# Gate stage of a mixer-and-experts kernel: load order of rows, state weights and last weight tiles; block 1's rows copied straight to the mixer's tile

## What is computed

```
xn  = (x - mean(x)) / sqrt(var(x) + eps)                       # row by row
mixer(xn):  proj = xn @ W_in.T                                 # 512 -> 2 x 1024
            u = silu(conv4(proj[:1024]) + conv_b); g = proj[1024:]
            h[t] = 0.95 h[t-1] + 0.05 (u @ W_B.T)[t]           # 64 states
            y = (h @ W_C.T + D * u) * silu(g)
            layernorm(y @ W_out.T + xn, ln_gamma, ln_beta)
experts(xn): scores = (tanh(xn @ gate_w.T) + 1) / 2            # 8 experts
            each expert takes its 1024 best rows: layernorm, fc1, gelu, fc2,
            times the score, added back to xn's rows
out = x + mixer(xn) + experts(xn)
```

## Time and profile before

| | us |
|---|---|
| median of 3 runs | 2635.19 (2635.17 to 2637.68) |
| the profiled execution's own time | 2637.41 |
| its span, first to last instruction | 2635.5 |
| PE (matmul) busy | 2606.3 |
| DVE busy | 2079.5 |
| ACT busy | 1481.2 |
| POOL busy | 675.0 |

### The profile page before, as it was taken

How to read it: one execution, slowest core, us unless ns; L and a number is a source line. 1 busy time by engine, 2 the same in 40 slices (tenths; PEclk the granted TensorE clock), 3 DMA queues, 4 the chain that set the end, 5 groups by cost and what they waited for, 6 DMA issues and landing times.

```text
span 2635.5 us, 38833 instructions
## 1 busy us (share of the span) xinstructions
PE 2606.3 (99%) x11592; PEld 2112.6 (80%) x11592; DVE 2079.5 (79%) x3570; ACT 1481.2 (56%) x2536; POOL 675.0 (26%) x1006
## 2 busy tenths in 40 slices
PE   8999999999999999999999999999999999999998
PEld 4588888888888888888888888888888888888886
DVE  8778888888888888887877778878788787887754
ACT  5744545555455656655544555565555655556553
POOL 5422222222222222213533213223132231312101
PEclk9999999999999999999999999999999999999999
DMA  9733222233333222335447436364363643636313
GB/s 367 265 128 111 76 92 87 89 104 112 112 112 112 79 85 85 96 104 166 136 125 195 109 117 161 92 155 127 117 160 93 153 131 115 159 92 156 98 56 72
DMA packets 262638, 329.62 MB, mean 125 GB/s; under 512 B 142032, under 2 KB 142160, under 8 KB 258640
## 3 DMA queue, kind: packets, MB, share of 16 engines
q1 hardware_dynamic: 228816, 230.91, 28.2%
q0 software_dynamic: 33664, 96.75, 14.9%
HBM read 259.14 MB, written 68.45 MB: 124 GB/s over the span
## 4 chain that ended last, share of the span: by engine, by line
PE 85%; DVE 10%; issue 2%; ACT 1%; DMA 1%; SPq 0%; POOL 0%; DVEq 0%; POOLq 0%; ACTq 0%
PE ring L1584 9%; PE ring L1585 9%; PE ring L1586 9%; PE po L2564 5%; PE po L2565 5%; PE po L2566 5%; PE po L1622 4%; PE pb L2565 4%; PE pb L2566 4%; PE pb L2564 4%; PE po L1623 4%; PE po L1624 4%; PE pc L2565 2%; PE pc L2566 2%; PE pc L2564 2%
## 5 line engine op out<-in xcount | busy, mean ns | idle before, releaser
L1584 PE MATMUL ring<-xt_h,w_h 128*128 128x512 f32 x1024 | 400.1, 391 | 0.1
L2564 PE MATMUL po<-w2h,hid_h 128*128 128x512 f32 x1024 | 399.3, 390 | 0.8
L1585 PE MATMUL ring<-xt_l,w_h 128*128 128x512 f32 x1024 | 398.5, 389 | 0.0
L2565 PE MATMUL po<-w2l,hid_h 128*128 128x512 f32 x1024 | 398.5, 389 | 0.0
L1586 PE MATMUL ring<-xt_h,w_l 128*128 128x512 f32 x1024 | 398.4, 389 | 0.0
L1373 DVE SCALAR_TENSOR_TENSOR u<-xin,cw,u 128x512 f32<-128x512 f32 x384 | 288.4, 751 | 75.9 <-issue 47.0
L2041 POOL DMA_INDIRECT out_dram<-res,idx_c x64 | 105.0, 1640 | 495.0 <-DVE res L2411 483.5
L2564 PEld LDWEIGHTS po<-w2h,hid_h 128*128 128x128 f32 x1024 | 192.2, 188 | 43.9 <-DVE hid_l L2401 3.8
L1584 PEld LDWEIGHTS ring<-xt_h,w_h 128*128 128x128 f32 x1024 | 192.2, 188 | 41.0 <-DVE xt_l L542 0.9
L1586 PEld LDWEIGHTS ring<-xt_h,w_l 128*128 128x128 f32 x1024 | 192.2, 188 | 40.1
L2565 PEld LDWEIGHTS po<-w2l,hid_h 128*128 128x128 f32 x1024 | 192.2, 188 | 39.6
(11 more groups left out here) (301 smaller groups left out, 6263.1 us busy)
## 6 DMA issues: line engine op xcount, KB each, us to landing
w2r<-fc_in SPq DMA_DIRECT2D x256, 256.0 KB
wo<-wo_halves POOLq DMA_DIRECT2D x120, 512.0 KB, 4.5
w1r<-fc_in SPq DMA_DIRECT2D x144, 256.0 KB
x_tail<-x_in SPq DMA_DIRECT2D x64, 256.0 KB, 2.8
out_dram<-res SPq DMA_DIRECT2D x64, 256.0 KB, 2.0
g_x<-x_in SPq DMA_DIRECT2D x15, 1024.0 KB, 8.5
xt_rows<-g_xnt SPq DMA_DIRECT2D x15, 1024.0 KB, 10.2
rows<-xt_rows SPq DMA_DIRECT2D x15, 1024.0 KB, 6.3
```

What stands on the lines that cost most here:

```text
L1584: pe.matmul(ring[r % 2][:, :], w_h[:, r, q], xt_h[:, k, :], start=(k == 0), stop=False)
L1585: pe.matmul(ring[r % 2][:, :], w_h[:, r, q], xt_l[:, k, :], start=False, stop=False)
L2564: pe.matmul(dst, ah, bh, start=start, stop=False, skip_group_check=more)
L2565: pe.matmul(dst, ah, bl, start=False, stop=False, skip_group_check=more)
```

## The change

The order of blocks becomes 2 to 15, then 1, then 0. Turn 14 (block 1) is evicted into `next_x` itself, and the products read it there; its store and the load in front of the mixer go, and the counts of stores and row loads are changed to match. SP loads the state weights behind the last x load and the last store of the group of turns 8 to 11, then the convolution's weights, then the last four tiles of W_in, which were loaded one by one in that group; then two stores; then the two row vectors, which have a count of their own that POOL and DVE wait for ahead of mixer turn 1. ACT makes the three halves of the state weights and rounds the last four tiles behind all turns; POOL subtracts for the last four tiles behind the state weights' low parts; DVE scales W_B behind its last turn. PE's last group is written out rather than looped, and in mixer turn 0 step r waits for the low part of tile r instead of all 16.

```diff
 def at(b):
-        return 0 if type(b) is int and b == NB - 1 else b + 1
+        return NB - 1 - b if type(b) is int and b >= NB - 2 else b + 2
+
+    def evicted(b, i):
+        return next_x if type(b) is int and b == NB - 2 else xnt[i]
...
                 load_x(NB - R + i if last else b + R, i)
                 store_xt(b, i)
-                load_raw(NB - R + i if last else b + R, i)
+                if not last:
+                    load_raw(b + R, i)
...
+        group(NG - 2, last=True)
         sp.dma_start(staged2[0:S, 0:2, :], t["w_c"]).then_inc(c_win, 16)
         sp.dma_start(staged2[S:P, 0:2, :], t["w_c"]).then_inc(c_win, 16)
         sp.dma_start(staged2[:, 2, :], t["w_b"]).then_inc(c_win, 16)
-        group(NG - 2, last=True)
         sp.dma_start(w.cw[:, :, :], t["conv_w"]).then_inc(c_win, 16)
         sp.dma_start(w.cb[:, :], t["conv_b"]).then_inc(c_win, 16)
         sp.dma_start(w.dp[:, :], t["d_param"]).then_inc(c_win, 16)
-        sp.dma_start(ends.gamma[:, :], t["ln_g"].to_broadcast([P, D])).then_inc(c_win, 16)
-        sp.dma_start(ends.beta[:, :], t["ln_b"].to_broadcast([P, D])).then_inc(c_win, 16)
         for i in range(R):
-            if i < R - 1:
-                store_xt(NB - R + i, i)
+            load_raw(NB - R + i, i)
+        for i in range(R - 2):
+            store_xt(NB - R + i, i)
+        sp.dma_start(ends.gamma[:, :], t["ln_g"].to_broadcast([P, D])).then_inc(c_first, 16)
+        sp.dma_start(ends.beta[:, :], t["ln_b"].to_broadcast([P, D])).then_inc(c_first, 16)
...
         for i in range(R):
             turn(NB - R + i, i)
-            w_low(NB - R + i - 1, (i - 1) % R)
-        w_low(NB - 1, R - 1)
+            if i == 0:
+                w_low(NB - R - 1, R - 1)
         pool.wait_ge(c_sh, 2 + 1)
         pool.tensor_tensor(w.wc_lh[0:S, :], staged2[0:S, 0:2, :].rearrange("p a b -> p (a b)"),
                            f(w.wc_hh[0:S, :]), ALU.subtract).then_inc(c_sl, 1)
         pool.wait_ge(c_sh, 3 + 1)
         pool.tensor_tensor(w.wb[:, :, S:2 * S], staged2[:, 3, :].rearrange("p (c s) -> p c s", s=S),
                            f(w.wb[:, :, 0:S]), ALU.subtract).then_inc(c_sl, 1)
+        for i in range(R):
+            w_low(NB - R + i, i)
...
-        dve.wait_ge(c_win, 48 + 1)
+        group(NG - 1, last=True)
+        dve.wait_ge(c_win, 96 + 1)
         dve.tensor_scalar(staged2[:, 3, :], staged2[:, 2, :], INPUT_FACTOR, None,
                           ALU.mult).then_inc(c_id, 1)
-        group(NG - 1, last=True)
...
-        with pe.Fori(1, NG) as h:
+        with pe.Fori(1, NG - 1) as h:
             group(h)
+        group(NG - 1)
...
                 b = h * R + i
-                if last and i == R - 1:
-                    w_high(b, h, i)
-                if not first:
+                if not first and not (last and i == R - 2):
                     act.wait_ge(c_xs[i], h * 16 + 1)
                 for k in range(KD):
                     act.wait_ge(c_t, b * KD + k + 1 + 1)
-                    act.copy(xnt[i][:, k, :], pt[k][:, :]).then_inc(c_tc, 1)
+                    act.copy(evicted(b, i)[:, k, :], pt[k][:, :]).then_inc(c_tc, 1)
                     if last and i == R - 1:
                         act.copy(ew.yt_h[0][:, k, :], pt[k][:, :]).then_inc(c_th, 1)
                 if not (first and i == 0):
                     turn_tanh(act, b - 1)
+                if not last:
+                    w_high(b, h, i)
                 if not (last and i == R - 1):
-                    w_high(b, h, i)
                     normalise(b + 1, (i + 1) % R)
-                if last and i < 3:
-                    small_high(i)
                 act.wait_ge(c_se, (b + 1) * KD + 1)
                 act.wait_ge(c_sc, b + 1)
                 act.copy(sc_t[:, :], pst).then_inc(c_sr, 1)
+            if last:
+                for i in range(3):
+                    small_high(i)
+                for i in range(R):
+                    w_high(h * R + i, h, i)
...
-        load_rows(1)
         sp.wait_ge(sums.c_in_low, NW + 1)
...
         ls.constants(pool, c_set, 6)
+        pool.wait_ge(sums.c_row_in, 16 * 3 + 1)
...
         turn(0, False, bisect_0)
+        dve.wait_ge(sums.c_row_in, 16 * 3 + 1)
...
                 pe.wait_ge(c_tl, (b + 1) * KD + 1)
-                if type(b) is int and b == 0:
-                    pe.wait_ge(sums.c_in_low, NW + 1)
+            if type(b) is int and b == 0:
+                pe.wait_ge(sums.c_in_low, r + 1 + 1)
```

More of the change, by code:

```diff
@@ L278, in stage_gate @@
     w_h, w_l = ew.w1, ew.w2
+    next_x = ew.rows
     begun = len(m.counts.counts)
@@ L292, in stage_gate @@
     c_t = sums.c_gate_t
-    c_tc = m.count("g_tc")
+    c_tc = sums.c_gate_out = m.count("g_tc")
     c_th, c_tl = sums.c_th, sums.c_tl
@@ L307, in stage_gate @@
     c_xa = m.count("g_xa")
-    c_first = m.count("g_first")
+    c_first = sums.c_row_in = m.count("g_first")
     c_x = [m.count(f"g_x_in{i}") for i in range(R)]
@@ L570, in group @@
                     pe.wait_ge(c_tc, b * KD + k + 1 + 1)
-                    pe.matmul(pst, gw[:, k, :], xnt[i][:, k, :], start=(k == 0),
+                    pe.matmul(pst, gw[:, k, :], evicted(b, i)[:, k, :], start=(k == 0),
                               stop=(k == KD - 1)).then_inc(c_se, 1)
@@ L594, in small_high @@
             if i == 0:
-                act.wait_ge(c_win, 48 + 1)
+                act.wait_ge(c_win, 96 + 1)
                 act.copy(w.wc_hh[:, :], staged2[:, 0:2, :].rearrange("p a b -> p (a b)")).then_inc(c_sh, 1)
@@ L1080, in sync @@
         for i in range(4):
-            sp.wait_ge(sums.c_xt_store[i], 16 * (NB // 4 - i // 3) + 1)
-        load_rows(1)
+            sp.wait_ge(sums.c_xt_store[i], 16 * (NB // 4 - i // 2) + 1)
         sp.wait_ge(sums.c_in_low, NW + 1)
@@ L1215, in t_high @@
             if k == 0:
-                act.wait_ge(c_rows, 16 * (b + 1) + 1)
+                if type(b) is int and b == 0:
+                    act.wait_ge(sums.c_gate_out, (NB - 1) * KD + 1)
+                else:
+                    act.wait_ge(c_rows, 16 * b + 1)
                 act.wait_ge(c_ag, (b + 1) * NW + 1)
@@ L1342, in turn @@
                 ends.normal_rows(act, b, k)
-        act.wait_ge(sums.c_small_in, 16 * 8 + 1)
+        act.wait_ge(sums.c_small_in, 16 * 6 + 1)
         act.wait_ge(sums.c_small_low, 2 + 1)
@@ L1347, in scalar @@
         for i in range(4):
-            act.wait_ge(sums.c_xt_store[i], 16 * (NB // 4 - i // 3) + 1)
+            act.wait_ge(sums.c_xt_store[i], 16 * (NB // 4 - i // 2) + 1)
         act.wait_ge(c_set, 6 + 1)
@@ L1357, in vector @@
     def vector(dve):
-        dve.wait_ge(sums.c_small_in, 16 * 8 + 1)
+        dve.wait_ge(sums.c_small_in, 16 * 6 + 1)
         dve.wait_ge(c_set, 6 + 1)
```

## The result

| | before | after |
|---|---|---|
| median, us | 2635.30 (8 runs, 2635.17 to 2638.47) | 2644.47 (8 runs, 2643.36 to 2645.09) |
| ratio, 95% interval | | 1.0030 (1.0021 to 1.0039) |
| profiled execution, us | 2637.41 | 2644.86 |
| its span, us | 2635.5 | 2642.9 |

The changed kernel is slower, by 9.2 us between the medians (0.35%), by 8.1 us between the means (2636.2 and 2644.3 us, to which the ratio of 1.0030 is close), by 7.4 us between the two profiled executions. Most of the difference between these numbers is in the kernel before: five of its runs lie at 2635.2 to 2635.4 us, three at 2637.2 to 2638.5 us, and the profiled one is of the second sort.

What follows compares the result with a forecast made beforehand. PE, busy for 99% of the span, was taken as the bound. A gain of 1.85 us and a shift of 9.0 us summed to +7.15 us: 2644.6 us profiled, 2642.3 us by the median; range 2638.8 to 2646.3 us.

Steps and rivals of the forecast that it cites:

- case A: Whole kernel: the forecast itself, 2641 to 2644 us, chance 0.66.
- Load order: Gate stage: state weights and last four tiles behind the x loads cut PE stalls, gain 1.85 us, bounds 0 and 2.0.
- The rule on GpSimd's and VectorE's common interfaces: Gate stage, turns 13 to 15: DVE about 0.96 us faster per turn without w_low; without the rule, gain 0.3 us lower.
- turn 13's stall: Gate stage, PE's 0.27 us stall ahead of turn 13: can't return, by the rule on GpSimd's and VectorE's contention.
- Copy to place: Gate stage: block 1's store and load back go, nobody waited for them, 0 us.
- ACT's tail: Behind the last score copy: ACT's work ends 5.1 us after the last products; alone, step 2 would be 0.3 us late.
- POOL's tail: Seam into the mixer: memsets done 11.8 us after the last products, 7.1 us of PE idle time, bounds 6.5 and 7.8.
- The clock: After the PE gap: half clock for some 4 us from the restart, 1.9 us lost, bounds 0 and 3.5.
- That rule of the Trainium skill: PE after the gap: a wait can lower the array's clock, the next burst starts cold; without it, 1.4 us less.
- rival B: After the PE gap: the clock stays up, shift 7.6 us, sum +5.75 us, 2640.9 us, chance 0.14.
- Nothing won back: Mixer behind the first share of u: PE has no slack, so the 9.0 us shift stays.

Runs made afterwards that it cites:

- state_ahead: The changed kernel with the three state weight loads put back in front of the group of turns 8 to 11; 2645.1 us.
- copy_only: The kernel before with block order 2 to 15, 1, 0 and block 1 evicted to its place, without its store and load; 2637.9 us.
- scale_late: The kernel before with DVE's scaling of W_B moved behind its last group, nothing else; 2636.8 us.
- low_behind4: The changed kernel with POOL's four last weight subtractions (w_low) moved behind the mixer's memsets and first edge copies; 2642.6 us.
- busy_gap: The changed kernel with 28 idle matmuls on PE behind mixer step 1, in the gap; 2642.8 us.
- memsets_first: The changed kernel with the mixer's memsets and first edge copies on POOL ahead of the state weights' low halves and four w_low; 2640.7 us.
- low_behind2: The changed kernel with two of POOL's four last weight subtractions moved behind the mixer's memsets; 2644.8 us.
- early_tail: The changed kernel with ACT's state halves and roundings in turns 13 to 15, POOL's subtractions following, DVE's W_B scaling behind its turn 13; 2637.0 us.
- tiles_ahead: The changed kernel with the last four weight tiles' loads put back between the x loads of turns 12 to 15; 2645.5 us.
- seam_only: The kernel before, loads and block order kept, with only the change's ACT and POOL order behind the last scores and mixer step r's finer wait; 2645.5 us.
- early_tail2: As early_tail, but the three small convolution loads counted with the row vectors, so turn 13 waits for w_c and w_b alone; 2636.7 us.

## Why the prediction was right

It said 2642.3 us and slower by 0.27%; measured were 2644.5 us and a ratio of 1.0030, inside its range. The mechanism is that of case A, which it held likeliest, but the median lies 0.5 us above A's 2641 to 2644, and the half clock lasted longer than A had it. Step by step:

- **Load order.** 1.85 us of gain was taken, 1.97 us measured from turn 8 to T, no stall ahead of turns 11 to 13. The share of each cause was simpler in the text than on the chip: it put all on 0.75 MB ahead of x, and state_ahead shows 0.6 us from that alone. A further 0.3 us was lost before turn 8 (61.15 against 60.81 us), in the start's variation. The rule on GpSimd's and VectorE's common interfaces (Trainium skill, GPSIMD Engine Reference, 8. Key points) was borne out twice: 1.45 us for the normalisations without `w_low`, and 5.00 instead of 2.32 us for a convolution beside it. But turn 13's stall did not hang on it, as the prediction had it: in copy_only and scale_late it was gone with `w_low` in place.
- **Copy to place.** 0 was taken; copy_only's total was no different from before, 0.4 us less in the gate stage.
- **ACT's tail.** Taken to end at T+5.1, measured T+5.4; not the bound. low_behind4 shows that without the `w_low` the gap is 2.04 us, which is POOL's low halves (T+2.8 to T+6.4) with the memsets behind them (0.4 us), and not ACT's roundings.
- **POOL's tail.** Memsets done at T+11.8 by the sum, at T+11.6 by the trace; gap 7.1 against 6.92 us; 1.2 us of gap for each `w_low`, as the runs with 4, 2 and 0 of them show.
- **The clock.** The fall came inside the gap, as taken. The term was too small: 1.9 us by 4 us at half clock, where it was 4.9 us and 2.4 us lost (busy_gap gets 2.25 of them back). That rule of the Trainium skill (TensorE: Matmul & The Clock Gate, HAM oscillation — how this bites in real kernels), that a wait can throw the array back to the lower clock, is what the windows at 119.00 and 120.50 us show; rival B, in which the clock stayed up, fell.
- **Nothing won back.** From the first share to the last the distance is 23.2 us before and 23.1 after. PE's last matmul starts at 2631.96 us, at 2624.02 before: 7.94 us later, just as the first share did (128.48 against 120.59, 7.89 us).

The sum of the terms was +7.15 us; the same terms as measured are -1.63 (T) and +9.5 (seam), +7.9 us. That the profiled execution, 2644.86 us, came within 0.3 us of the 2644.6 that the sum gave is in part luck: the span grew by 7.4 us only, since what lies behind PE's last matmul took 10.9 instead of 11.5 us, for which no run shows a reason. The means differ by 8.1 us, 0.2 more than the terms. Against the medians 1.3 us more are missing. The quicker start, which most runs of the kernel before may have had and its profiled one had not, would give that; those runs left no trace, so it stays open.

## What to carry to other kernels

Ask of every instruction put at the end of a stage what the next stage's first instructions on the same engine are, and who waits for them: six memsets of 0.4 us, behind four subtractions whose results PE first uses in mixer step 12, over 30 us later, held ACT, DVE and PE for 7 us. POOL's work that is moved out of such a seam has to go where DVE, which it holds up here, is idle, or much of the gain is lost as DVE's delay. And a gap on PE can cost more than its length: here another 2.4 us of half clock, which idle matmuls in the gap avoided.

## What the runs showed that was not expected

POOL's subtraction of a 128x512 tile and DVE's instructions with two SBUF inputs hold each other up almost wholly: 2.68 us more for three DVE instructions and 1.45 us more for four on POOL in low_behind4, 2.87 and 0.5 us in memsets_first. In low_behind4 the seven ended 6.36 us after the first had begun; alone they take 4.91 + 2.32 = 7.23 us. low_behind2 gave back nearly all of the 3.3 us that its shorter gap had won, about half through this and half through the clock behind it.

The start of the kernel is itself of two kinds, whatever the version. PE has a gap ahead of turn 1. In the profiles where it lasted 1.6 to 2.2 us (early_tail, scale_late, state_ahead, tiles_ahead, memsets_first, low_behind4) the granted clock stayed at 1.00, and turn 8 began at 58.5 to 59.7 us. Where it lasted 2.4 to 3.1 us (before, after, seam_only, low_behind2, busy_gap, copy_only, early_tail2) some 3.4 us at 0.50 followed, and turn 8 began at 60.8 to 61.3 us. This is as large as the spread of the runs, and as the gain that early_tail2 was after.
